# A graph network kernel: the attention loop's DVE and PE work in another order, sixteen pairs of count scatters put behind the loop, constant products on PE

## The reference

```python
# layer 0, the one that this change touches: two GAT convolutions, 4 heads of 64 and 8 heads of 32
def _gat_conv(x, src, dst, W, a_src, a_dst, bias, heads, out_ch, n_nodes):
    h = (x @ W).reshape(n_nodes, heads, out_ch)
    alpha_s = jnp.einsum('nhc,hc->nh', h, a_src)
    alpha_d = jnp.einsum('nhc,hc->nh', h, a_dst)
    e = jax.nn.leaky_relu(alpha_s[src] + alpha_d[dst], negative_slope=0.2)
    m = jax.ops.segment_max(e, dst, num_segments=n_nodes)
    ex = jnp.exp(e - m[dst])
    denom = jax.ops.segment_sum(ex, dst, num_segments=n_nodes)
    a = ex / (denom[dst] + 1e-16)
    msg = h[src] * a[:, :, None]
    out = jax.ops.segment_sum(msg, dst, num_segments=n_nodes)
    return out.reshape(n_nodes, heads * out_ch) + bias
x_cat = jax.nn.elu(jnp.concatenate([out1, out2], axis=-1))
result = residual + x_cat @ Wu + bu
```

## Time and profile before

| | us |
|---|---|
| median of 3 runs | 3968.54 (3967.72 to 3983.3) |
| the profiled execution, its own time | 3979.62 |
| its span, first to last instruction | 3978.0 |
| TensorE clock granted, mean | 0.86 |
| busy: PE, DVE, POOL, ACT | 3256.7, 2287.9, 2121.5, 1316.3 |
| attention loop, first to last transfer on POOL | 264.0 to 1763.8 |
| unify stage | 1784.6 to 1873.2 |

### The profile page before, as it was taken

The page is one execution under the profiler, slowest core; times in us unless marked ns, Lnnn a source line. Parts: engine busy times, 40 slices in busy tenths (PEclk is TensorE's granted clock), DMA queues, the critical chain, the costliest instruction groups (busy, mean ns, idle before and its releaser), DMA issues. The chain is left out here.

```text
span 3978.0 us, 63564 instructions
## 1 busy us (share of the span) xinstructions
PE 3256.7 (82%) x15679; PEld 2207.9 (56%) x15680; DVE 2287.9 (58%) x7089; ACT 1316.3 (33%) x3037; POOL 2121.5 (53%) x1867
## 2 busy tenths in 40 slices
PE   7267888788887888766898989898969788988978
PEld 4145655555555665545555555555544566666644
DVE  8856777777777777759313131313252566766768
ACT  0123333333333333323413131313155545555522
POOL 0356888888888788850363636362000066766710
PEclk9886777777777677768899999999979899999989
DMA  6249556555656556642453535353239344444420
GB/s 258 47 129 296 136 136 141 137 136 141 137 136 141 136 136 141 140 76 41 133 183 114 181 114 181 108 184 108 90 89 271 91 132 123 129 120 124 125 54 22
DMA packets 471407, 528.87 MB, mean 133 GB/s; under 512 B 191947, under 2 KB 376489, under 8 KB 471223
## 3 DMA queue, kind: packets, MB, share of 16 engines
q0 software_dynamic: 141664, 236.21, 24.3%
q1 hardware_dynamic: 316938, 271.68, 23.6%
q10 hardware_dynamic: 12749, 20.33, 1.4%
HBM read 437.02 MB, written 70.53 MB: 128 GB/s over the span
## 5 line engine op out<-in xcount | busy, mean ns | idle before, releaser
L1065 PE MATMUL p_out<-rows,hot 128*128 128x266 f32 x2048 | 829.1, 559 | 36.4 <-DVE rows L1184 29.3
L990 POOL DMA_INDIRECT count_dram<-number,place x384 | 647.6, 1686 | 152.4 <-issue 116.1
L1065 PEld LDWEIGHTS p_out<-rows,hot 128*128 128x128 f32 x2048 | 519.6, 273 | 234.5 <-DVE rows L1184 128.9
L1605 POOL DMA_INDIRECT rec_dram<-records,edge_place x416 | 405.5, 975 | 437.7 <-PE p_hi L1638 224.3
L982 POOL DMA_INDIRECT rows<-att_dram,idx x512 | 540.3, 1055 | 163.7 <-issue 122.1
L1534 PE MATMUL p_lo<-cbuf,parts 128*128 128x400 f16 x1750 | 581.8, 332 | 0.0
L1535 PE MATMUL p_hi<-cbuf,parts 128*128 128x400 f16 x1750 | 581.8, 332 | 0.0
L2115 POOL DMA_INDIRECT col_rows<-col_dram,m_idx x440 | 416.7, 947 | 249.5 <-issue 143.8
L1562 DVE TENSOR_TENSOR node_sum<-p_hi,low_sb 128x400 f32<-128x400 f32 x80 | 45.9, 574 | 572.6 <-ACT low_sb L1553 572.6
L1184 DVE TENSOR_TENSOR rows<-rows 128x512 f32<-128x512 f32 x512 | 349.2, 683 | 0.2 <-ACT rows L951 0.2
L1048 PE MATMUL p_top<-rhs,hot 128*128 128x17 f32 x1024 | 178.3, 310 | 136.7 <-DVE rhs L1123 136.7
(11 more groups left out here) (394 smaller groups left out, 5952.0 us busy)
## 6 DMA issues: line engine op xcount, KB each, us to landing
cbuf<-count_dram SPq DMA_DIRECT2D x40, 2500.0 KB
dl_rep<-dl_dram SPq DMA_DIRECT2D x128, 256.0 KB
count_dram<-zeros SPq DMA_DIRECT2D x20, 1000.0 KB, 21.2
g_rows<-count_dram SPq DMA_DIRECT2D x25, 800.0 KB, 4.7
rec_dram<-blank ACTq DMA_DIRECT2D x1, 17600.0 KB, 72.7
m_group_rows<-rec_dram SPq DMA_DIRECT2D x110, 160.0 KB, 2.3
records<-in_edges POOLq DMA_DIRECT2D x32, 520.0 KB, 5.5
key_rep<-key_dram SPq DMA_DIRECT2D x64, 256.0 KB
```

Of the source, the lines that this page charges most:

```text
L990: nc.gpsimd.indirect_dma_start(count_dram, bass.IndirectOffsetOnAxis(ap=place[r][:, n, c:c + 1].bitcast(U32), axis=0), number[r][:, 2 * n ...
L1065: m = nc.tensor.matmul(p_out[q][:, side, 0:HALF], hot[k][:, u, :], rows[k][:, u, side * HALF:(side + 1) * HALF], start=(u == 0), stop=(u = ...
L1605: nc.gpsimd.indirect_dma_start(rec_dram, bass.IndirectOffsetOnAxis(ap=edge_place[:, at:at + 1].bitcast(U32), axis=0), records[b % 3][:, j, ...
```

## The change

Five things are changed, all around the attention loop.

1. DVE: `run_up` is for group j+2 and stands near the end of `work(j)`, behind `if_first`; `weigh` of step 3 stands behind `new_top`; the third `alike` stands behind `top_of`.
2. PE: `turn` is for group j+2 and stands behind the first three `add_up`; the wait for `added` stands first.
3. PE: `keep_clock`, products of `ident_bf` with a constant of 240 columns into columns 272 to 511 of the two `p_out` banks, which nobody reads. It is called with 2 at the group's start, behind `turn_back`, ahead of each of the first three `add_up`, ahead of `look_up`, and ahead of the last `add_up`.
4. In turns 0 to 15 the second pair of the group k = 2 is not scattered; DVE writes its places and numbers into `place_late` and `number_late`. The turns are 10 scatters long there (`issued`). DVE and POOL have two loops for this in place of one.
5. Those 16 pairs are scattered later: 4 at the end of the loop's block, 12 in the unify stage; none are left for the two calls behind. The wait for all scatters moves from the loop's end to the transposition stage.

```diff
+LATE_ROUNDS, LATE_ATT, LATE_UNI, LATE_NORM = 16, 4, 16, 16
+        def scatter_late(pool, first, last):
+            for n in range(first, last):
+                pool.wait_ge(late_made, 2 * n + 2)
+                pool.wait_ge(placed, (CH - 2 * LATE_ROUNDS + 2 * n) * 16)
+                pool.nop().then_inc(waits_passed, 1)
+                for c in range(2):
+                    nc.gpsimd.indirect_dma_start(
+                        count_dram, bass.IndirectOffsetOnAxis(ap=place_late[:, n, c:c + 1].bitcast(U32), axis=0),
+                        number_late[:, 2 * n + c:2 * n + c + 1], None, compute_op=ALU.add).then_inc(placed, 16)
...
+        def issued(k, i, late):
+            return i * (BODY - 2) + (PRE + (0, 4, 6, 8)[k]) if late else i * BODY + (PRE + PARTS[k][0] - 2 * LATE_ROUNDS)
...
-                            if k % 2 == 0:
+                            if second:
                                 pair(k, 1, before + 2)
-                            else:
+                            elif k % 2 == 1:
                                 pair(k, 0, before)
...
-                        rounds(pool, work)
-                        pool.wait_ge(placed, CH * 16)
+                        rounds_in_two(pool, work)
+                        scatter_late(pool, 0, LATE_ATT)
                         pool.wait_ge(blank_out, 16)
...
+                        def keep_clock(k, n, fresh=False):
+                            for i in range(n):
+                                nc.tensor.matmul(p_out[k % 2][:, i % 2, 272:], ident_bf[:], mask[:, 1, 0:240], start=fresh, stop=True,
+                                                 skip_group_check=True)
+
                         def work(j, k, tiles):
-                            if within(j, 1):
-                                turn(j + 1)
-                                turn_back(j + 1)
-                                node_tops(j + 1, (k + 1) % 4)
                             if not (isinstance(j, int) and j < 2):
                                 pe.wait_ge(added, j - 1)
+                            keep_clock(k, 2, True)
+                            if within(j, 1):
+                                turn_back(j + 1)
+                                keep_clock(k, 2)
+                                node_tops(j + 1, (k + 1) % 4)
                             for u in range(U - 1):
+                                keep_clock(k, 2)
                                 add_up(j, k, u)
+                            if within(j, 2):
+                                turn(j + 2)
                             if within(j, 1):
+                                keep_clock(k, 2)
                                 look_up(j + 1, tiles[k])
+                            keep_clock(k, 2)
                             add_up(j, k, U - 1)
...
+                            if late and k == 2:
+                                TT(place_late[:, bass.ds(i, 1), :], place_f[:, 1:2, :], own_place[:].unsqueeze(1), ALU.add).then_inc(late_made, 1)
+                                nc.vector.tensor_copy(number_late[:, bass.ds(i * 2, 2)], number[2][:, 2:4]).then_inc(late_made, 1)
...
                             n = o.did(TT(zz[:], p_tab[:, :, 0:HW], slots(k), ALU.add))
-                            if ahead:
-                                run_up(j + 1, 1 - q, i1 * 2 + k1 // 2)
                             o.need(n)
...
-                            weigh(j, k, 3)
...
                             new_top(j + 1, tile_after)
+                            weigh(j, k, 3)
                             n = o.did(if_first(j + 1, k1, i1))
+                            if within(j, 2):
+                                run_up(j + 2, q, (i + (k + 2) // 4) * 2 + (k + 2) % 4 // 2)
                             o.need(n)
-                            at_place(k1)
+                            at_place(k1, i1, late)
...
+                    @block.gpsimd
+                    def _(pool):
+                        scatter_late(pool, LATE_ATT, LATE_UNI)
...
+                @block.gpsimd
+                def _(pool):
+                    scatter_late(pool, LATE_NORM, LATE_ROUNDS)
+                    pool.wait_ge(placed, CH * 16)
```

More of the change, by code:

```diff
@@ L837, in rounds, with rounds_in_two @@
                 work(GROUPS - 4 + k, k, GROUPS // 4 - 1)
+        def rounds_in_two(engine, work):
+            for k in range(4):
+                work(k, k, 0, True)
+            for first, last, late in ((1, LATE_ROUNDS, True), (LATE_ROUNDS, GROUPS // 4 - 1, False)):
+                with engine.Fori(first, last) as i:
+                    for k in range(4):
+                        work(i * 4 + k, k, i, late)
+            for k in range(4):
+                work(GROUPS - 4 + k, k, GROUPS // 4 - 1, False)
+        def issued(k, i, late):
+            return i * (BODY - 2) + (PRE + (0, 4, 6, 8)[k]) if late else i * BODY + (PRE + PARTS[k][0] - 2 * LATE_ROUNDS)
         def within(j, ahead):
@@ L992, in pair, with work @@
                                     number[r][:, 2 * n + c:2 * n + c + 1], None, compute_op=ALU.add).then_inc(placed, 16)
-                        def work(j, k, i):
+                        def work(j, k, i, late):
                             ahead = within(j, 3)
-                            r, before = (k + 3) % 4, i * BODY + PRE + PARTS[k][0]
+                            r, before = (k + 3) % 4, issued(k, i, late)
+                            second = k == 0 or (k == 2 and not late)
                             pool.wait_ge(place_ready, j + 1)
@@ L1091, in _ @@
                         look_up(0, read_registers(nc, group_table, 0, 1, ET.PE, NT - 1)[0])
+                        turn(1)
                         body(0, False)
@@ L1149, in new_top, with alike @@
                             TT(flat(tab[:, bass.ds(tile, 1), HW:]), best[:], best[:], ALU.max).then_inc(hi_ready, 1)
-                        def alike(g, k, i, n):
+                        def alike(g, k, i, n, late):
                             first, count = PARTS[k]
                             if n == 0 and not (isinstance(g, int) and g < 4):
-                                dve.wait_ge(placed, i * (BODY * 16) + (PRE + first + count - BODY) * 16)
+                                before = PRE + (-6, -4, -2, 0)[k]
+                                dve.wait_ge(placed, i * ((BODY - 2) * 16) + before * 16 if late else
+                                            i * (BODY * 16) + (before - 2 * LATE_ROUNDS) * 16)
                             one = STT(same[:, n, :], key_rep[k % 2][:, n // 2 * 2:n // 2 * 2 + 2, :].rearrange("p u e -> p (u e)"),
@@ L1197, in add_sums, with work @@
                             TT(own, own, p_out[q][:, :, 0:HALF], ALU.add).then_inc(added, 1)
-                        def work(j, k, i, tile_before, tile_after):
+                        def work(j, k, i, tile_before, tile_after, late=False):
                             o.enter(j)
@@ L1267, in _ @@
                         for n in range(PARTS[0][1]):
-                            alike(0, 0, 0, n)
+                            alike(0, 0, 0, n, True)
                         o.link(if_first(0, 0, 0))
-                        at_place(0)
+                        run_up(1, 1, 0)
+                        at_place(0, 0, True)
                         o.begin(PER)
@@ L1274, in _ @@
                         for k in range(4):
-                            work(k, k, 0, tiles[k], tiles[k + 2])
-                        with dve.Fori(1, GROUPS // 4 - 1) as i:
-                            tiles = read_registers(nc, group_table, i * 4 - 1, 6, ET.DVE, NT - 1)
-                            for k in range(4):
-                                work(i * 4 + k, k, i, tiles[k], tiles[k + 2])
+                            work(k, k, 0, tiles[k], tiles[k + 2], True)
+                        for first, last, late in ((1, LATE_ROUNDS, True), (LATE_ROUNDS, GROUPS // 4 - 1, False)):
+                            with dve.Fori(first, last) as i:
+                                tiles = read_registers(nc, group_table, i * 4 - 1, 6, ET.DVE, NT - 1)
+                                for k in range(4):
+                                    work(i * 4 + k, k, i, tiles[k], tiles[k + 2], late)
                         tiles = (*read_registers(nc, group_table, GROUPS - 5, 5, ET.DVE, NT - 1), None)
@@ L1455, in clear_tables @@
                 nc.gpsimd.memset(ewT[:], 0.0).then_inc(ew_zero, 1)
+                scatter_late(pool, LATE_UNI, LATE_NORM)
             def load_tables(sp):
```

17 lines of the change are left out of this document (10 added, 7 removed).

## The result

The changed kernel took 3937.19 us in the median (3929.27 to 3943.29, 6 runs) against 3972.62 us (6 runs) of the kernel before on the same chip: ratio 0.9901 [0.9884, 0.9918], 35 us faster, where 39 were forecast. The profiled execution has a span of 3941.3 us against 3978.0, 36.7 less.

The account below looks back on a forecast made before the run. POOL's transfers were taken to bound the loop, 11.35 us a group. Terms -63.7 + 21 + 2 + 2 gave -39 us, so 3930 us from the runs' median 3968.54; its own range 3896 to 3955, overall 3893 to 3966.

Parts of the forecast that it names:

- The bound: Attention loop: POOL's 28 indirect transfers a turn set the pace, 45.4 us a turn or 11.35 us a group.
- The term of -63.7: First 16 turns: 32 scatters leave the loop, each taking its 1.99 us along; a turn becomes 41.4 us.
- The new code of the second loops (+2): Entering the second DVE and POOL loops needs new code: +2 us, range 0 to 6, an estimate.
- The new order: DVE and PE in the loop: worth nothing alone, up to 0.2 us in each of 64 groups once scatters are gone.
- The products: PE in the loop: 14 a group at 0.106 us raise the clock above 0.85, which by itself returns nothing.
- The end: Loop's end: four late pairs, 6.0 us apart, queue behind the last scatter's landing and cost +21 us, range 2 to 25.
- The unify stage: Twelve late pairs hide in the 89 us stage with some 18 us to spare, but slow DVE by +2 us.
- The 37 us: Unify stage: by an exclusive DVE-GpSimd port lock, 24 scatters of 1.55 us could hold DVE 37 us.
- A (more comes back): All rounds speed up and the loop's end costs under 10 us: about -65 us, 3904 us; chance 0.10.
- B (PE becomes the bound): Products do not raise the clock; PE needs 12.2 us a group against 11.35: some +130 us, 4098; chance 0.10.
- C: Late pairs exposed: each lands slowly at the end (55 to 70 us), or DVE is held (+37): about 3965; chance 0.14.
- D (DVE's chain at 10.9): DVE's chain sits at 10.9 us a group or more, so early groups gain 0.45 at most: -6 us, 3963; chance 0.08.

Follow-up runs that it names:

- the four kernels on chip C: Changed kernel (3939.95 us), it without constant products (3950.15), it with 28 products a group (3930.46), it with no late pairs at loop's end and dropped entries 64 bytes apart (3904.08).
- the spread: Changed kernel with the addresses of dropped scatter entries 64 bytes apart in place of 2: 4202.82 us, ratio 0.9932 to the kernel before, chip A.
- the kernel with nothing at the end: Changed kernel with late pairs twelve in unify, two in norm, two in transposition, none at loop's end, and dropped entries 64 bytes apart: 3904.08 us, ratio 0.9815, chip C.

## Why the prediction was right

**The bound.** Right. POOL's 32 scatters left, and the turn shrank by nearly what they took, 3.7 us of 4.0 (45.9 to 42.2 on the mean of turns 4 to 16): 28 transfers to 26. The order and the products alone bring nothing (753.8 us for turns 1 to 16), the late pairs do (the two were compared on chip A, not on the result's). The term of -63.7 came out at -61.4 in the first profile; the transfers that stay are 14 and 5 ns longer and their gaps 0.01 to 0.02, so that a turn is 42.1 us; the forecast's 41.4 also started from one turn of 45.4, where the mean is 45.9. Not all of it is a steady turn's: the second turn fell from 60.3 to 54.1 us and the first from 47.3 to 42.5, the other fourteen by 3.6 each. Those first two gave 11.0 of the 61.4 us, which no term of the sum had; why they were longer before is not shown, and that the term came so close is partly luck.

**The second half.** +6.3 was not forecast. In the four kernels on chip C the same fifteen turns took 684.3 to 690.8 us, the kernel before 687.9; so 694.2 is most likely one execution's spread. The start's -5.8 was not forecast either: 264.0 before, 258.2 to 262.8 in all profiles since, ahead of any changed code; with one profile of the kernel before, it stays open whether that is spread. The two nearly cancel, which is luck. The new code of the second loops (+2) was a guess without a row, and no run shows it: the turn at their start takes 45.2 us, the shortest of the half.

**The new order.** "Worth nothing by itself, up to 0.2 us in each of 64 groups" is what the runs gave: nothing without late pairs, 9.7 and 13.8 us with them, by one profile each on chips A and B. One step of its reasoning was wrong: DVE's wait for `p_in` does not go. It was 0.71 us a group, it is 18.5 us in 38 groups, 0.49 each, and has moved with `run_up` to the place ahead of `at_place`, where POOL does not feel it. The wait before `absent` fell from 0.29 to 0.09 us.

**The products.** The clock came out over 0.85 as said (0.90 in the turns). That it returns nothing while POOL has 28 transfers a turn is shown by the kernel with order and products only. For the short turns "returns nothing" was too strong on chip C: 3 us of turns and 10 us in the median for 14 products, with overlapping intervals, and 19.7 us in the median for 28, clear of noise. My price of a product, 0.106 us, was right (0.10). The group's own work at full clock, 7.4 us, was too large, since it adds up instructions that overlap: the rows of chip C give 6.6 to 6.7. The error was on the safe side, and PE's cycle stayed below POOL's.

**The end.** +21 and +21.6, with the parts shared out otherwise than I wrote. Pairs are 5.7 us apart, not 6.0. The "20 us between" that I read as landing plus barrier, 22.4 us from the last scatter's start to DVE's, are some 14 us by which the landing is slow and which the spread takes away, and 8.8 us for all else. The late pairs wait for it once, and the last of them lands without delay, so the sum stays the same: 18.55 + 3 x 5.67 + 1.85 + 7.55 = 45.0 us from the last scatter's start to DVE's, 22.4 before.

**The unify stage.** +2 was too much: +0.2 with 24 scatters (94.6 us in the kernel with nothing at the end, which has 24 there too). DVE's clamp in the loop kept its durations, which answer to the earlier trace rows, and in the unify stage the division, with two inputs in SBUF, took 683 ns in the median as against 682:

```profile
L1261 DVE TENSOR_SCALAR zz<-zz x128: 180/195/540, 278.7 to 1697.3; 128x64 f32<-128x64 f32 x128
...
L1395 DVE TENSOR_TENSOR val<-acc,den x25: 677/683/686, 1749.3 to 1821.5; 128x512 f32<-128x512 f32 x25
```

What the meeting cost fell on POOL: the 24 scatters took 41.96/24 = 1.75 us each, up to 2.14, where those at the loop's end took 1.55. The Trainium skill, SBUF — State Buffer (section SBUF: two separate sides), has the lock between DVE and GpSimd narrower than the prediction told it: on DVE's side it is for an instruction in a two-port mode, or with two SBUF inputs beside a GpSimd instruction that reads SBUF. The 37 us that the prediction drew from it, DVE shut out for every scatter, do not agree with the stage's 94.1 us and the division's 677 to 686 ns. That is shown for this kind of transfer alone.

My margin was nearly used up all the same. The second pair there waits 17.94 us for the landing of the first, and the last scatter starts at 1831.08, some 8 us ahead of the stage's end, where I had put the end of all twelve pairs 18 us ahead of it. The sign that the prediction named, late pairs more than 7.4 us apart, came true for that one step. Beside that wait stands a transfer of SP, `dinv_dram`, started at 1745.43 and landed 17.6 us later:

```profile
dinv_dram<-dinv SPq DMA_DIRECT2D x1, 12.5 KB, 17.6
```

The wait is also there with the dropped entries apart and nothing at the loop's end (19.02 us), so it isn't theirs. In that profile other transfers that SP started within 3 us of the same moment landed as late:

```profile
fold_wi<-in_m_W_ihT SPq DMA_DIRECT2D x1, 768.0 KB, 19.7
fold_w<-in_m_W SPq DMA_DIRECT2D x1, 256.0 KB, 19.4
...
dinv_dram<-dinv SPq DMA_DIRECT2D x1, 12.5 KB, 19.6
```

Which of them holds the scatters up, if it is one of them, was not tested.

**The rivals.** A (more comes back) is out: the end costs what it was priced at. B (PE becomes the bound) is out: even 28 products do not make it so. C is half there: one slow landing, for another reason than assumed, and paid once; DVE isn't held. D (DVE's chain at 10.9) did not occur on the chip of the result. On chip B the groups are at 11.1 us and the change gains nothing, which is D's size, but with late sums of PE and not by DVE's own chain. The range was wide: its end at 3966 us is 2.5 us under the 3968.54 of no change, so it held D too.

## What to carry to other kernels

Work that is taken off the engine that sets the pace is worth nearly its full time, gaps between instructions included, until the next engine's cycle is reached. Put it down where that engine has nothing to do, and count the places by the pair, for four pairs at a barrier gave back a third of what sixteen had won. Look at the wait in front of every barrier by what it moves: here 14 us of it were additions to unread places side by side. Don't read the price of an added instruction from the difference in busy time when the clock differs too. And measure a gain of 1% on more than one chip: it was 1.0% where it was first measured and on chip C, and nothing on chip B.

## What the runs showed of the hardware

- An indirect scatter with addition whose entries nearly all go to neighbouring two-byte places lands some 14 us later than one with its places 64 bytes apart (first late pair 18.55 us behind the last scatter's start in the changed kernel, 3.83 with the places apart on chip A; the next stage 22.4 us behind it in the kernel before, 8.8 with the places apart on chip C).
- A scatter of 128 two-byte additions costs POOL 1.55 us at the loop's quiet end and 1.70 on the mean in the loop, and a gap of 0.30; pairs that wait for each other's landing follow each 5.7 us there and each 6.1 in the unify stage. Beside them DVE lost nothing that shows (stage of 94.1 us against 93.9).
- 14 products of 240 columns a group took TensorE's granted clock over turns 1 to 16 from 0.73 to 0.92 in the first two profiles, and 28 took it to 0.98 on chip C (0.75 with none), at 0.10 us a product at full clock; PE was busy 9.5 us of a 10.4 us cycle with 28.
- On two chips on which everything behind the unify stage was about a tenth slower, the short turns of the new order mostly took 44 to 45 us, with the products and without them; on one of them the changed kernel's clock was at half for 3.3 and 6.8 us in each turn looked at.
